# A first phase of dense products over four source batches instead of three, in a fused two-layer graph kernel

## What is computed

```python
h = maximum(layernorm(x), 0)
msgs = einsum('ni,roi->rno', h, W0)[edge_type, src]        # layer 1
x = x + segment_sum(msgs, dst) + b0
h = maximum(layernorm(x), 0)                               # layer 2
h2 = h @ W1
out = segment_sum(dinv[src] * dinv[dst] * h2[src], dst) + b1
x = x + leaky_relu(out, 0.2)
```

## Time and profile before

| | |
|---|---|
| median of three runs | 2737.76 us |
| the profiled execution's own time | 2734.91 us |
| its span in the profile | 2729.9 us |
| TensorE matmul busy | 2163.5 us (79%) |
| TensorE weight load busy | 1888.1 us (69%) |
| VectorE busy | 1278.5 us (47%) |
| ScalarE busy | 1626.5 us (60%) |
| GpSimd busy | 1638.8 us (60%) |
| mean granted TensorE clock | 0.912 |

### The profile page before, as it was taken

How to read it: one execution, slowest core, us unless ns; L and a number is a source line. 1 busy time by engine, 2 the same in 40 slices (tenths; PEclk the granted TensorE clock), 3 DMA queues, 4 the chain that set the end, 5 groups by cost and what they waited for, 6 DMA issues and landing times.

```text
span 2729.9 us, 44783 instructions
## 1 busy us (share of the span) xinstructions
PE 2163.5 (79%) x14284; PEld 1888.1 (69%) x14284; DVE 1278.5 (47%) x3606; ACT 1626.5 (60%) x3915; POOL 1638.8 (60%) x1735
## 2 busy tenths in 40 slices
PE   2466677777787788788877888889999989868798
PEld 2355666766677677677766777777777777757677
DVE  8235546555555655655556552222222233423358
ACT  5335656565675667567666765566575655645541
POOL 5566666656656666655555656666666666666614
PEclk9578888888898889899989999999999999989899
DMA  8334444444554454646555646555454444544546
GB/s 284 83 94 123 125 124 145 137 119 133 159 152 135 142 171 134 197 144 180 180 159 155 214 140 211 166 152 147 126 152 126 138 125 127 140 115 116 132 85 182
DMA packets 385415, 400.73 MB, mean 147 GB/s; under 512 B 243699, under 2 KB 299296, under 8 KB 385056
## 3 DMA queue, kind: packets, MB, share of 16 engines
q0 software_dynamic: 78832, 215.52, 27.7%
q1 hardware_dynamic: 260816, 137.09, 18.2%
q10 hardware_dynamic: 45536, 45.26, 4.9%
HBM read 320.75 MB, written 76.96 MB: 146 GB/s over the span
## 4 chain that ended last, share of the span: by engine, by line
PE 58%; issue 12%; ACT 11%; another core or an unknown queue 8%; DVE 5%; ACTq 1%; POOL 1%; DMA 0%; DVEq 0%; POOLq 0%; SPq 0%
PE ps_slot L1636 21%; PE ps_slot L1696 11%; PE ps_proj L1650 10%; PE ps_aux L1696 9%; PE ps_slot L1664 7%; ACT staged_f L1311 4%; ACT gap_f L1376 3%; ACT wide_f L1369 2%; ACT onehot_f L1384 2%; DVE hots_f L1541 1%; DVE hots_f L1538 1%; PE ps_slot L1715 1%; POOL rows_f L1132 1%; DVE acc_f L1454 1%
## 5 line engine op out<-in xcount | busy, mean ns | idle before, releaser
L1132 POOL DMA_INDIRECT rows_f<-table,idxT x1612 | 1533.4, 951 | 942.2 <-issue 401.1
L1636 PE MATMUL ps_slot<-onehot_f,rows_f 128*128 128x128 f32 x6448 | 951.8, 299 | 175.8 <-issue 86.5
L1636 PEld LDWEIGHTS ps_slot<-onehot_f,rows_f 128*128 128x128 f32 x6448 | 889.2, 211 | 214.6 <-issue 163.3
L1311 ACT ACTIVATE staged_f<-ps_slot 128x400 uint8<-128x400 f32 x800 | 359.9, 500 | 432.4 <-remote 275.0
L1376 ACT ACTIVATE gap_f<-iota,keyT 128x128 bf16<-128x128 bf16 x1614 | 526.6, 393 | 58.3 <-ACT staged_f L1311 28.7
L1538 DVE TENSOR_TENSOR hots_f<-ps_slot,keys_f 128x400 bf16<-128x400 bf16 x800 | 288.3, 360 | 529.4 <-remote 320.3
L1664 PE MATMUL ps_slot<-hots_f 128*128 128x100 bf16 x3200 | 261.1, 219 | 249.2 <-issue 127.7
L1384 ACT ACTIVATE onehot_f<-gap_f 128x384 f32<-128x384 bf16 x538 | 276.6, 514 | 249.4 <-remote 145.9
L1664 PEld LDWEIGHTS ps_slot<-hots_f 128*128 128x128 bf16 x3200 | 210.3, 117 | 308.4 <-issue 271.9
L1650 PE MATMUL ps_proj<-w0t,acc_f 128*128 128x256 f32 x1600 | 381.0, 389 | 14.0 <-issue 12.7
L1454 DVE TENSOR_TENSOR acc_f<-ps_slot,acc_f 128x256 f32 x538 | 227.4, 423 | 349.6 <-remote 153.5
(11 more groups left out here) (157 smaller groups left out, 942.7 us busy)
## 6 DMA issues: line engine op xcount, KB each, us to landing
stash_f<-table SPq DMA_DIRECT2D x25, 1280.0 KB
rows_f<-table,idxT POOLq DMA_INDIRECT x1612
abuf_f<-counts_d SPq DMA_DIRECT2D x71, 320.0 KB
table<-hs_f SPq DMA_DIRECT2D x47, 256.0 KB
table<-xres SPq DMA_DIRECT2D x10, 640.0 KB, 6.7
acc_f<-x_d SPq DMA_DIRECT2D x50, 128.0 KB, 2.6
x_d<-xt_f SPq DMA_DIRECT2D x49, 128.0 KB
xt_f<-in_x_dram SPq DMA_DIRECT2D x48, 128.0 KB
```

The costliest lines, as they stand in the source:

```text
L1132: eng.indirect_dma_start(rows0[:, k, c, :], None, V["table0"], bass.IndirectOffsetOnAxis(ap=idxT[:, n * LOT + c:n * LOT + c + 1], axis=0)) ...
L1311: eng.activation(staging[:, h % 2, :, (w % HSUB) * SUB:(w % HSUB + 1) * SUB], count_bank(w)[:, 0:SPAN * MW].rearrange("p (d t) -> p t d", ...
L1636: last = eng.matmul(o[:, b * W:(b + 1) * W], rows0[:, k, c, b * P:(b + 1) * P], onehot[:, n % HOTS, c, :], start=(c == 0), stop=(c == chun ...
```

## The change

One constant changes; everything else follows from it through the planner.

```diff
-FIRST_BATCHES = 3
+FIRST_BATCHES = 4
```

## The result

The changed kernel takes 2736.35 us (median of 20 runs), beside 2742.3 for the kernel before, also from 20 runs: a ratio of 0.9975, interval [0.9966, 0.9984]. That is 6 us faster, where 10 were forecast. Measured again on two chips, with 12 runs each, the ratio was 1.0003 [0.9989, 1.0017] and 1.0001 [0.9992, 1.0010]. So it is a gain of 0.25% in one measurement and none that can be told from no change in two.

A forecast was written before the change was run, and what follows sets the result against it. The count round of VectorE, TensorE and ScalarE was taken to set the pace until the counts end, TensorE nearly the bound after. Terms -8 - 2 - 1 + 0 + 1 = -10 us took 2737.76 to 2728 us, range 2715 to 2746.

The forecast's parts named there:

- Lots 206 to 241, forecast -8: Taking 12 of 15 dense pieces out leaves the count round: 172.1 to 173.6 us instead of 181.2, 8 us gained.
- the excess belongs to this stretch's other work: Bound of 0 gain for lots 206 to 241, if other work that stays, above all the key search, makes them slow.
- the 35 us of TensorE: Matmul time of the 12 pieces leaving lots 206 to 241; beside the count round, so not itself the gain.
- The colder clock: Emptied lots 206 to 241 clock lower, 0.87 instead of 0.91: 5 us more busy time, possibly leaving a gain of 3.
- Lots 242 to 285, forecast -2: Six stash loads become one or two, gaining 5 us; the 3072 KB move falling here costs 3; net gain 2.
- the move, priced at 3: The 3072 KB move now falls in lots 242 to 285; taken as 3 us, between bounds 0 and 8.
- Lots 286 to 362, forecast -1: Same dense pieces, nine stash loads become five: a gain of 1 us, bounds 0 and 5.
- Lots 484 to 527, forecast +1: 11 postponed pieces, some 29 us of TensorE, hide in 45 us where it stands; 1 us lost, upper bound 29.
- The prediction's own sign of being wrong: The two windows from lot 206 to 285 together not falling by at least 5 us.
- B: No change: dense work is nearly free or a colder clock eats the gain; 2735 us, within 2733 to 2739; chance 0.22.
- A: Lots 484 to 527 give the gain back: 11 postponed pieces add up to 29 us there; 2747 us; chance 0.19.
- C: Stash loads are the main cost, nearly 2 us each by holding up gathers and widenings; 18 us gained, 2720; chance 0.14.

The follow-up runs named there:

- hold_238: The kernel before, with groups 6 to 11 not allowed to start before slot 238 and the move kept at slot 208; 0.9987, then 1.0000 of before.
- experiment 7: The move cut from 3072 KB to 64 KB, in the kernel before and in the changed kernel; 1.0032 and 1.0045 of the kernel before.
- experiment 5: The kernel before, with the rows of 13 stash loads copied once more to unused DRAM beside each load; 1.0002 of before.

## Why the prediction was at best right in direction, and wrong in size

- **Lots 206 to 241, forecast -8: this step failed.** Measured on late chips: a mean of 178.5 for the order of before and 178.9 for the changed one, so 0; on prompt chips 146.5 and (mean of four) 146.9. Two things failed: the reference was wrong, and a cost stood nowhere in the sum. I priced an emptied lot at 4.78 to 4.82 us from windows of 44 lots, in each of which a key search is spread over 44; here one whole search falls on 36. Even the kernel with no dense work from slot 213 to 320 needs 175.1 us (4.86 per lot), so some 3.4 us were to be had there. I had named this bound ("the excess belongs to this stretch's other work") and chosen a value near the reference instead. And the restart takes even that: the emptied lots did get faster, lots 206 to 227 by 3.2 us on late chips (107.6 to 104.4, `hold_238` taken in) and 8.6 on prompt ones (88.2 to 79.6), and lots 228 to 241 got slower by 4.0 (70.9 to 74.9) and 9.0 (58.3 to 67.3). There TensorE waits 4.2 to 5.6 us for the copied keys, with a piece at half the clock behind it. On the prompt chips the longer wait (5.55 against 1.72 us) and the slow piece (4.61 against 2.54) make 6 of the 9 us; waits of 3.0 to 7.2 us for gathered rows stand beside them. That the 35 us of TensorE are not the gain was sound. What the restart costs beside the key copy stood in the sum at nothing. The colder clock came as the Trainium skill's rule says (TensorE: Matmul & The Clock Gate, "The HAM clock gate"): 0.91 to 0.88.
- **Lots 242 to 285, forecast -2: larger.** 216.3 to 211.5 on late chips, so -4.8, and 172.0 to 170.6 on prompt ones, so -1.4. The 5 us put down to fewer stash loads would fit the late chips if the move, priced at 3, cost nothing at its new place. But the loads are not shown to be the cause: held to 238, with four loads, the stretch takes 211.7 and 210.8 as well, and doubled traffic costs nothing that shows. (The bounds of +8 and -4 don't follow from the terms either: a gain of 5 less 0 to 8 gives +5 to -3.)
- **Lots 286 to 362, forecast -1:** on late chips +1.5 and -1.4, so 0. On prompt chips -6.4 and +2.2, each to 0.7 us in the profiles of the table, which no step foresaw.
- **Lots 484 to 527, forecast +1: right in mechanism and size.** 197.5 to 197.1 in the first two profiles, and 195.8 against 194.3 and 193.5 on other late chips; 160.2 and 162.3 on prompt ones against 159.5, 159.8 and 162.4.
- **The sum.** On late chips lots 206 to 362 come to 748.2 (mean of three, 743.3 to 752.7) and 743.8 (mean of two), -4.4 us or 0.16%, between the two ratios measured there (0.9975 and 1.0003), but inside the scatter of one kernel. On prompt chips lots 206 to 537 took 1259.0 and 1259.2 us in one pair of profiles, 1264.9 and 1256.9 in the pair of experiment 7. The prediction's own sign of being wrong was a fall of less than 5 us in lots 206 to 285: they fell 7.2 us in the first two profiles, and from 394.8 to 390.4, so 4.4, over all late ones. That the first ratio came near the forecast is luck: its largest term brought nothing, and the gain stands in lots 242 to 285 for a cause that is not shown. The first issue of L1196 came at 1388.39 us, not near 1360.
- **Rivals.** B (no change; only 2 to 3 us from fewer batch changes) is what two of three measurements show. A is real on prompt chips at 4 of its 29 us. C is refuted in its mechanism by experiment 5.

Open: why the ratio was 0.9975 in one measurement and 1.0003 and 1.0001 in two; what in the order of the pieces makes lots 242 to 285 one to nine us shorter, and why lots 286 to 318 answer on one kind of chip only.

## What to carry to other kernels

- Price an emptied stretch from a stretch with the same side work per lot, not from a mean of longer ones: here a search comes once in 48 lots.
- Work that is taken out of a stretch starts again somewhere. Look at what the engines do in just that lot: here it met a key copy, and a wait of 4.2 to 5.6 us stands where the emptied lots' gain was lost.
- Work that is hidden cost a fraction of its busy time here (0.05 of 0.28 us), and its removal brought back no more.
- A change of 0.2% needs several profiles and more than one chip: lots with identical instructions differed by 7 us between two profiles.

## What was not expected of the hardware

The same program took 2712 us on two chips (2742 in the first measurement) and 2269 and 2273 on two others, 16% less, with the same durations on ScalarE, VectorE and GpSimd. TensorE's matmuls last 393 and 391 ns in the median (L1696), but its granted clock is 0.912 to 0.916 and 0.958. The largest difference found in the traces is how long after the last matmul TensorE's signals are recorded (median 1.7 to 2.1 us against 0.29); that it makes the whole 16%, and the lower clock with it, is argued from the waits and not tested. On prompt chips the gathers are a part of the bound: GpSimd's share of the chain rises to 17%, as this page line of the kernel before on a prompt chip shows, and windows behind lot 285 repeat to 0.1 us (137.3 and 158.4 in three profiles).

```profile
PE 57%; POOL 17%; issue 8%; ACT 6%; DVE 5%; DMA 3%; ACTq 0%; DVEq 0%; POOLq 0%; SPq 0%
```
